# Transformer passes of a macaron block: a new order of work on every engine, t1 kept twice, q with a Newton chain of its own

## The reference, cut to what matters

```python
def shift_tokens(t):                       # second half of the features comes from the token before
    a, s = jnp.split(t, 2, -1)
    s = jnp.pad(s, ((0, 0), (1, 0), (0, 0)))[:, :-1]
    return jnp.concatenate([a, s], -1)

def attn_layer(x, Wqkv, qs, ksc, Wo):      # 16 heads of 64
    q, k, v = split_heads(x @ Wqkv)
    q = l2norm(q) * qs
    k = l2norm(k) * ksc
    q = q * cos * scale + rotate_half(q) * sin * scale
    k = k * cos * inv + rotate_half(k) * sin * inv
    out = local_attention(q, k, v)         # windows of 32, each sees itself and the one before
    return merge(out) @ Wo

def ffn_layer(x, g, bln, W1, b1, W2, b2):
    mu = x.mean(-1, keepdims=True)
    var = ((x - mu) ** 2).mean(-1, keepdims=True)
    xn = (x - mu) / jnp.sqrt(var + 1e-05) * g + bln
    a, gate = jnp.split(xn @ W1 + b1, 2, -1)
    return a * jax.nn.gelu(gate, approximate=False) @ W2 + b2

for i in range(DEPTH):                     # 6
    x = attn_layer(shift_tokens(x), Wqkv[i], q_scale[i], k_scale[i], Wo[i]) + x
    x = ffn_layer(shift_tokens(x), ln_g[i], ln_b[i], W1[i], b1[i], W2[i], b2[i]) + x
```

## Time and profile before

| what | value |
|---|---|
| median of 3 runs | 8010.39 us (8007.4 to 8014.43) |
| the profiled execution, its own time | 8002.75 us |
| its span (first to last instruction) | 8001.0 us |
| mean granted PE clock | 0.775 of full |
| busy PE / DVE / ACT / POOL | 74% / 74% / 39% / 30% |
| the two transformer passes | about 60 to 2322 us and 5285 to 7547 us |

### The profile page before, as it was taken

The page is one execution under the profiler, slowest core; times in us unless marked ns, Lnnn a source line. Parts: engine busy times, 40 slices in busy tenths (PEclk is TensorE's granted clock), DMA queues, the critical chain, the costliest instruction groups (busy, mean ns, idle before and its releaser), DMA issues. The chain is left out here.

```text
span 8001.0 us, 181736 instructions
## 1 busy us (share of the span) xinstructions
PE 5922.6 (74%) x65140; PEld 4101.7 (51%) x65140; DVE 5921.2 (74%) x27619; ACT 3146.3 (39%) x7946; POOL 2435.5 (30%) x2297
## 2 busy tenths in 40 slices
PE   6888888888866666666666666668888888888687
PEld 3444444444446565655656565634444444444444
DVE  5777777777757777777777777767777777777566
ACT  3555555555532222222222222235555555555311
POOL 4555555555510000000000000035555555555200
PEclk9999999999975555555555555579999999999888
DMA  1000000000000000000000000000000000000000
GB/s 41 1 15 12 4 12 4 12 4 1 1 4 2 2 2 2 2 2 2 2 2 2 2 2 2 2 27 1 15 4 12 12 4 12 4 1 2 8 2 12
DMA packets 31493, 50.74 MB, mean 6 GB/s; under 512 B 2191, under 2 KB 24426, under 8 KB 28906
## 3 DMA queue, kind: packets, MB, share of 16 engines
q1 hardware_dynamic: 30158, 38.45, 1.5%
q10 hardware_dynamic: 412, 0.42, 0.0%
HBM read 37.81 MB, written 1.05 MB: 5 GB/s over the span
## 5 line engine op out<-in xcount | busy, mean ns | idle before, releaser
L1157 PE MATMUL g_bank<-hbuf,Wgates 128*128 128x2 f32 x2048 | 601.0, 363 | 1031.1 <-DVE hbuf L1245 977.7
L1157 PEld LDWEIGHTS g_bank<-hbuf,Wgates 128*128 128x128 f32 x2048 | 513.2, 311 | 1146.9 <-DVE hbuf L1245 1092.6
L1265 POOL TENSOR_TENSOR xB<-hbuf,xA 128x32 f32 x64 | 16.4, 256 | 2859.7 <-DVE hbuf L1245 2859.7
L1199 ACT ACTIVATE tg<-g_bank 128x2 f32<-128x2 f32 x1024 | 176.1, 172 | 1697.1 <-PE g_bank L1157 1697.1
L1219 DVE TENSOR_SCALAR sg<-es 128x4 f32<-128x4 f32 x1024 | 173.8, 170 | 554.1 <-ACT es L1201 554.1
L1169 PE MATMUL e_bank<-tg,Weg 128*128 128x2 f32 x2048 | 579.3, 352 | 0.0
L1141 PEld LDWEIGHTS s_bank<-hparts,Wparts 128*128 128x128 bf16 x12288 | 570.7, 117 | 0.0
L1169 PEld LDWEIGHTS e_bank<-tg,Weg 128*128 128x128 f32 x2048 | 515.1, 312 | 0.0
L1141 PE MATMUL s_bank<-hparts,Wparts 128*128 128x2 bf16 x12288 | 469.4, 165 | 0.0
L1236 DVE SCALAR_TENSOR_TENSOR no<-ex,iso,fno 128x1 f32<-128x1 f32 x2048 | 351.1, 212 | 3.7 <-issue 1.6
L1255 DVE SCALAR_TENSOR_TENSOR cn<-ex,sg,fcn 128x1 f32<-128x1 f32 x2048 | 352.1, 214 | 0.0
(11 more groups left out here) (579 smaller groups left out, 17371.6 us busy)
## 6 DMA issues: line engine op xcount, KB each, us to landing
Wqk0a<-in_L_ffn_Wqkv SPq DMA_DIRECT2D x3, 1024.0 KB
Wva<-in_L_ffn_Wqkv SPq DMA_DIRECT2D x6, 512.0 KB, 6.0
Woa<-in_L_ffn_Wo SPq DMA_DIRECT2D x6, 512.0 KB, 7.3
Wqk1a<-in_L_ffn_Wqkv SPq DMA_DIRECT2D x3, 1024.0 KB
Wqk0b<-in_L_ffn_Wqkv SPq DMA_DIRECT2D x3, 1024.0 KB
Wvb<-in_L_ffn_Wqkv SPq DMA_DIRECT2D x6, 512.0 KB, 6.0
Wob<-in_L_ffn_Wo SPq DMA_DIRECT2D x6, 512.0 KB, 7.2
Wqk1b<-in_L_ffn_Wqkv SPq DMA_DIRECT2D x3, 1024.0 KB
```

The source lines that it names most:

```text
L1157: pe.matmul(g_bank[j][:, s * B:(s + 1) * B], Wg[:, 3, 1, :], h, start=False, stop=True, skip_group_check=True).then_inc(g_done, 1)
L1199: act.activation(tg[:, :], g_bank[j][:, s * B:(s + 1) * B], ACT.Tanh).then_inc(tg_ready, 1)
```

## The change

It keeps every operation of the arithmetic and changes order, buffers and the Newton chains:

- The loop of each engine has another order of calls and one iteration more.
- t1 is there twice (by n % 2). `rotate_q` and `rotate_k` wait for the turn of the tile before the last one. t2 is there once for q and k together (1024 columns instead of 2048), so `rotate_q` waits for the k sum of the tile before and `rotate_k` for the q sum.
- `norms_q`: the chain of q alone, on 16 columns, ahead of `rotate_k`. `norms` is the chain of k, and in every second iteration it takes along the two variances of a feed-forward group (18 columns); the group's own chain and the copy of the variance go. ACT `variance` writes the variances beside k's sums.
- POOL scales q (`norm_q`) ahead of `add_k`.
- After `gelu`, ACT runs one small Exp, so that the Exp table is loaded there.
- `row_sums` and `invert` move from the end of an iteration to the start of the next, `attend` and `take_output` from tile i-3 to i-2.

```diff
+def norm_runs(n, N):
+    return NEWTON * (n if n < N else N + (n - N) // 2)
@@ tensor_program
     def values(n, w):
-        if w == 1 or w == 3:
+        if w == 1:
+            pe.wait_ge(s.pt_ready, 2 * n + 2)
+        if w >= 2:
             pe.wait_ge(s.v_ready, 4 * n + w)
-        if w == 2:
-            pe.wait_ge(s.pt_ready, 2 * n + 2)
...
     def rows(g):
         pe.wait_ge(s.fx_ready, 2 * g + 2)
         if g:
+            pe.wait_ge(s.f_prod, 3 * g)
...
+    def back(g):
+        pe.wait_ge(s.f_xn, GROUP * (g + 1))
+        if g:
             pe.wait_ge(s.f_x, g)
...
-    for i in range(N + 6):
+    for i in range(N + 7):
             project_q(new)
+            values(old, 0)
+            turn_output(last)
+        if not even and 0 <= g < G:
+            gates(g)
+            turn_probs(old, 0)
+            project_k(new)
             turn_q(now)
-            attend(last)
+            turn_probs(old, 1)
+        if even and 0 <= g < G:
+            rows(g)
+            values(old, 1)
             turn_k(now)
+        if even and 0 <= g - 1 < G:
+            contract(g - 1)
+            values(old, 2)
+            values(old, 3)
             score(now)
+            attend(old)
         if not even and 0 <= g < G:
+            lins(g)
         if even and 0 <= g < G:
+            back(g)
@@ vector_program
     def rotate_q(n):
         if n:
-            dve.wait_ge(s.q_turned, 2 * n)
-            dve.wait_ge(s.q_sum, n)
+            dve.wait_ge(s.k_sum, n)
+        if n >= 2:
+            dve.wait_ge(s.q_turned, 2 * (n - 1))
...
+    def norms_q(n):
         dve.wait_ge(s.q_ssq, n + 1)
         if n:
             dve.wait_ge(s.q_scaled, n)
+        rsqrt_steps(dve, s.q_newton, NEWTON * n, c.ssq[:, 0:HEADS], c.rnorm[:, 0:HEADS], c.ntmp[:, 0:HEADS], 1e-24, 0.0)
...
+    def norms(n, g):
+        if n < N:
+            dve.wait_ge(s.k_ssq, n + 1)
+        if g is not None:
+            dve.wait_ge(s.f_var, g + 1)
+        if n:
+            dve.wait_ge(s.k_scaled, min(n, N))
+        rsqrt_steps(dve, s.newton, norm_runs(n, N), c.ssq[:, HEADS:], c.rnorm[:, HEADS:], c.ntmp[:, HEADS:], 1e-24, 0.0)
...
+            row_sums(old)
+            invert(old)
         if even and 0 <= g - 1 < G:
             multiply(g - 1)
+            rotate_q(new)
+            residual(last)
+            squares_q(new)
+            norms_q(new)
             rotate_k(new)
+            statistics(g)
+            squares_k(new)
+            norms(new, g if even and 0 <= g < G else None)
             largest(now)
+            normalise(g, new)
             finish(g - 1)
@@ scalar_program
+        act.activation(c.scrap[:, :], c.ones[:, 0:1], ACT.Exp).then_inc(s.table_loaded, 1)
+
+    def variance(g, n):
+        act.wait_ge(s.f_aggr, GROUP * (g + 1))
+        act.wait_ge(s.newton, norm_runs(n, N))
+        act.activation(c.ssq[:, 2 * HEADS:], c.fmv[:, :, 1], ACT.Identity, bias=c.eps[:, :]).then_inc(s.f_var, 1)
...
+            exponent(old)
+            scale(g)
+            square_q(new)
+            take_values(old, 0)
+            take_probs(old, 0)
             square_k(new)
+            take_q(now)
+            take_probs(old, 1)
+            take_values(old, 1)
+            take_k(now)
+            variance(g, new)
+            take_values(old, 2)
+            take_values(old, 3)
+            gelu(g)
+            take_output(old)
         if layer + 1 < N // TILES and 6 <= j < 12:
@@ pool_program
+            norm_probs(old)
+            shift_rows(g)
             add_q(new)
             shift(new + 1)
+            norm_q(new)
             add_k(new)
+            move_k(new)
             norm_k(new)
@@ transformer
-        c.t1, c.t2, c.sq = (sb(x + nm, [P, 2 * INNER]) for x in ("t1", "t2", "sq"))
+        c.t1 = [sb(f"t1{i}" + nm, [P, 2 * INNER]) for i in range(2)]
+        c.t2, c.sq = sb("t2" + nm, [P, INNER]), sb("sq" + nm, [P, 2 * INNER])
```

More of the change, by code:

```diff
@@ L439, in turn_probs @@
         if pc == 0:
[L440 removed]
+            pe.wait_ge(s.v_ready, 4 * n + 1)
         else:
@@ L527, in contract @@
         for i, (at, w) in enumerate(FFC):
-            last = pe.matmul(fa[:, 0:GCOLS], c.W2[layer % 2][0:w, i, :], c.fh[0:w, i, :], start=(i == 0), stop=(i == 2))
+            last = pe.matmul(fa[:, GCOLS:], c.W2[layer % 2][0:w, i, :], c.fh[0:w, i, :], start=(i == 0), stop=(i == 2))
         last.then_inc(s.f_out, 1)
@@ L831, in scalar_program @@
         layer, j = divmod(i, TILES)
-        if new < N:
-            square_q(new)
-        if 0 <= now < N:
-            take_q(now)
-        if 0 <= last < N:
-            take_output(last)
-        if 0 <= old < N:
-            take_values(old, 0)
-        if 0 <= now < N:
-            take_k(now)
-        if 0 <= old < N:
-            take_values(old, 1)
+        if 0 <= old < N:
+            exponent(old)
         if not even and 0 <= g < G:
@@ L846, in scalar_program @@
         if new < N:
+            square_q(new)
+        if 0 <= old < N:
+            take_values(old, 0)
+            take_probs(old, 0)
+        if new < N:
             square_k(new)
+        if 0 <= now < N:
+            take_q(now)
         if 0 <= old < N:
-            take_probs(old, 0)
             take_probs(old, 1)
+            take_values(old, 1)
+        if 0 <= now < N:
+            take_k(now)
+        if even and 0 <= g < G:
+            variance(g, new)
+        if 0 <= old < N:
             take_values(old, 2)
-        if 0 <= now < N:
-            exponent(now)
+            take_values(old, 3)
+        if not even and 0 <= g < G:
+            gelu(g)
         if 0 <= old < N:
-            take_values(old, 3)
+            take_output(old)
         if layer + 1 < N // TILES and 6 <= j < 12:
@@ L860, in scalar_program @@
                 keep_weights(layer + 1, j - 8)
-        if not even and 0 <= g < G:
-            gelu(g)
 def pool_program(pool, c, s, N):
-    t1, t2 = c.t1, c.t2
+    t2 = c.t2
     def heads(a):
@@ L955, in pool_program @@
         layer, j = divmod(i, TILES)
-        if 0 <= now < N:
-            move_k(now)
+        if 0 <= old < N:
+            norm_probs(old)
+        if even and 0 <= g < G:
+            shift_rows(g)
         if new < N:
             add_q(new)
-        if even and 0 <= g < G:
-            shift_rows(g)
         if new + 1 < N:
@@ L964, in pool_program @@
         if new < N:
+            norm_q(new)
             add_k(new)
-            norm_q(new)
+            move_k(new)
             norm_k(new)
-        if 0 <= now < N:
-            norm_probs(now)
         if layer + 1 < N // TILES and 8 <= j < 12:
```

138 lines of the change are left out of this document (58 added, 80 removed).

## The result

The changed kernel takes 8075.1 us (median of four, 8066.4 to 8084.7), the kernel before beside it 8009.6: a ratio of 1.0081, 95% interval 1.0064 to 1.0099. It is slower by 0.8%; the forecast was 7915 us, 1.2% faster. The execution in the profile after took 8084.65 us, the longest of its four, and the one before 8002.75, so the traces lie 82 us apart where the medians lie 65 apart.

A forecast was written before the change was run, and what follows sets the result against it. Waits between engines, closing over turn_q, were taken as the bound. A pass: 47.5 x 44.35 + 44 - 13 = 2138 us against 2186.5; 95 less for two gives 7908, or 7915 as a median; range 7770 to 8060.

The forecast's parts named there:

- the ring that follows: New order up to the scores: take_values(2) waits behind take_k, values(3) and score behind it; largest at 15.44 us, odd iteration.
- the chains: Newton chains on DVE beside POOL's adds: q ends at 7.2 or 8.25 us, k at 14.5 (odd) or 15.65 (even).
- the walk: Sum of one iteration in the new order from rotate_q's start: 21.75 us odd, 22.6 even, 44.35 a pair against 46.0.
- back 19.31, project_q 19.58, and behind it on PE and ACT 1.98 and 1.02: End of an even iteration: back waits for finish, then project_q and square_q, giving the next rotate_q at 22.6 us.
- the 2.02 for project_k: Start of an iteration on PE: project_k starts at 2.41 us, square_k 2.02 us later, at 4.43.
- My own sign, a mean clock of 0.95 or more: Expected in the profile after if the forecast held: PE's clock at 0.95 or more.
- a rival at 17%: PE at half clock after idling before values(3): 2.5 us in even iterations, 119 a pass, 8150 in all; chance 0.17.
- PE had less idle time in a pair: Argument against the clock falling: less PE idle time in a pair of iterations, and 3.3 us waits for norm_q gone.
- 1.35 us for a join in an even iteration: Weight step ahead of the exponent in ACT's queue: 1.35 us more in even iterations, part of 44 us a pass.
- the variance: ACT's variance ahead of take_values(2) in even iterations, after DVE's statistics at 11.2 us: 0.2 more, largest at 15.62.
- 13 less: First four iterations of a pass lack work of older tiles: 13 us less a pass.
- The change cuts this ring: Kernel before: waits from rotate_q through norm_q and turn_q to the next rotate_q, t1 being there once; 46.0 us a pair.

The follow-up runs named there:

- e2: Changed kernel with unread identity transposes on PE: 8 ahead of project_k in even iterations, 8 ahead of values(old, 3), 14 ahead of back; 7952.6 us, ratio 0.9931.
- e3: Changed kernel with the weight step on PE behind attend, ahead of lins and back instead of behind them; 7929.6 us, ratio 0.9905.
- e4: Changed kernel with POOL's shift_rows behind add_q, as before the change; 8057.9 us, ratio 1.0069.
- e7: Changed kernel with q's own Newton chain undone: one chain of 34 columns, POOL's norm_q behind move_k; 8054.2 us, ratio 1.0047.
- e8: Kernel before with t1 twice and nothing else, so rotate_q and rotate_k wait for the turn two tiles back; 8008.1 us, ratio 0.9995.
- e10: Changed kernel: score ahead of values(3), gelu, weight step and lins earlier, shift_rows behind add_q, exponent ahead of take_output, q's own chain undone; 7724.7 us, ratio 0.9652.

## Why the prediction was wrong

**Right: the ring that follows.** The wait for take_values(2) behind take_k was named, and largest stands 0.13 us from its forecast place. Plain odd iterations are 21.8 (21.75), odd ones with weights 23.7 (23.6). That these get 4 us longer is no side effect: the exponent, row_sums and multiply, which were covered before, now stand between largest and the next rotate_q.

**Right: the chains.** The first steps of the q chain take 1.10 us and, in even iterations, 2.2 (1.1 and 2.1 said), that of the k chain 1.30 in odd ones (about 1) and 0.2 to 1.0 in even ones. DVE comes second in odd iterations and together with PE in even ones, as forecast. Two slips in the sums cost nothing: by the walk's own terms the k chain of an even iteration ends at 15.43, not 15.65, and finish at 19.38 (18.17 + 0.73 + 0.48), not 19.25. From largest to back the trace has 3.7 us, as the walk has.

**Wrong: the clock in the even iteration.** The step that failed is "back 19.31, project_q 19.58, and behind it on PE and ACT 1.98 and 1.02", and with it the 2.02 for project_k: both were taken at full clock. In the trace after, project_q took up to 3.78 us and was slow in 36 of 92 even iterations, project_k up to 3.78 and in 45 of 92; e2, where none is, puts the price at 122 us. My own sign, a mean clock of 0.95 or more, came true all the same (0.96). The clock was a rival at 17%, but I put its fall into the wait ahead of values(3). There the 64 products of the scores kept their 1.96 us in every iteration from the fifth on. I also reasoned that PE had less idle time in a pair. It has more: 9.8 us, from 8.2 before, the gaps between PE's rows in a pass, a pair's share of them; only the longest single wait fell, from 3.3 us and more to 2.1. Both waits in question, 1.4 us for rotate_q and 2.1 us for finish, have a long project right behind them, on which square, rotate and all the rest wait. Before, what ran at half clock was mostly attend (over 2.7 us in 88 of 192), with slack behind it. Why the clock falls in some even iterations and not in others with the same waits stays open.

**The same failure, at the weight step.** I took 1.35 us for a join in an even iteration, at full clock. In the trace after it costs 3.4 us (27.4 against 24.0), since the join, project_q and the exponent behind it are in one queue behind the longest wait. With the clock kept up, in e2, it costs 1.3 (24.4 against 23.1), as said. So this is no second mistake: it is in e2's 122 us, and e3 gets it by order.

**Mis-sized: the variance.** The walk gave it 0.2 us, and largest came 0.5 later than the walk in a plain even iteration (16.12 against 15.62). Of that 0.13 is there in odd iterations, too (15.57 against 15.44). The variance costs 0.3 instead of 0.2 even when the statistics are early: in e4 and e7 it starts straight behind take_k, at 11.2, and largest at 15.9. The last 0.24 are the late statistics, behind the q chain's step of 2.23 us. The half microsecond stays in e2 (23.1 against 22.6). Over 46 even iterations and two passes that is 46 us, and the first four iterations, for which "13 less" was too much, add some 5 a pass. In time e2 and the forecast lie less far apart (7952.6 and 7915), mainly because the stretch between the passes, which the walk left as it was, came out 10 us shorter: 3028.7 us from the last start of q in the first pass to the first in the second, 3038.9 before.

**Wrong in the first part: what bounded the kernel before.** "The change cuts this ring" was true of the semaphore and not of the time: e8 cuts it and gains nothing.

## What to carry to other kernels

When a wait is removed from a ring, walk the new order of all engines, but do it at both clocks of PE: here a project of 1.98 us behind a wait of 1.4 or 2.1 us took up to 3.8, and its place decided whether that cost anything. The mean clock did not show it (0.95 before, 0.96 after). In these queues written by hand, the next bound was never one queue: the bank, ACT's gelu and PE's attend lay within about 1 us of each other. Two of the single moves (25 and 17 us) and the wait cut alone (0) gave almost nothing, where e10, with all the moves and q's chain undone, gave 350 (8075.1 to 7724.7). The exception was the weight step, 146 us by itself: put work that nobody waits for into the longest wait rather than behind it.

## What the runs showed of the hardware

The clock was lost in waits that look alike: with 1.4 us of idle time before it, project_k took 3.61 us in one even iteration and 1.98 in another of the same trace. From the fifth iteration on, no wait of PE in these passes was longer than 2.2 us. Idle transposes in these waits held the granted clock at 1.00.

Both table loads of a group took 1.28 us on ACT, and nothing more came with them: in the odd iteration above, the load started at 6816.70 and the first gelu at 6818.00.

The Trainium skill, SBUF — State Buffer, section "SBUF: two separate sides", states that the pair of ports goes to whichever starts first, a POOL instruction or a DVE step in a two-port mode or with two SBUF inputs, and that the other is blocked; so the blocking can go both ways. The trace after shows both: POOL's second shift copy and the third step of the q chain start within 0.01 us of each other in 190 of 192 iterations. In half of them the copy takes 0.34 us and the step 0.17, in the other half the copy 0.29 and the step 0.32. These are the lines of one iteration of each kind:

```profile
6808.10 0.34 POOL L915 COPY xq0b<-xA 64x128 f32<-64x128 f32 x1
6808.10 0.17 DVE L87 TENSOR_SCALAR rnormb<-rnormb 128x16 int32<-128x16 int32 x1
...
6877.28 0.29 POOL L915 COPY xq3b<-xA 64x128 f32<-64x128 f32 x1
6877.28 0.32 DVE L87 TENSOR_SCALAR rnormb<-rnormb 128x16 int32<-128x16 int32 x1
```
